# Attention stage: two accumulator banks, row maxima in three single banks with one VectorE instruction each, and the rounding of the maxima on GpSimd

## The reference

```
qkv    = (h @ w_qkv + b_qkv).reshape(B, T, 3, 16, 16)       # B=4, T=1024, 16 heads of 16 channels
scores = einsum('bhqd,bhkd->bhqk', q, k) / sqrt(16)
attn   = softmax(scores, axis=-1)
out    = einsum('bhqk,bhkd->bhqd', attn, v)
```

## Time and profile before

| | us |
|---|---|
| median of three runs (1148.0 to 1151.61) | 1149.8 |
| the profiled execution, its own time | 1148.59 |
| its span, first to last instruction | 1146.5 |
| PE busy in the span | 1062.9 (93%) |
| DVE busy | 997.4 (87%) |
| ACT busy | 808.4 (71%) |
| POOL busy | 244.1 (21%) |

### The profile page before, as it was taken

The page is one execution under the profiler, slowest core; times in us unless marked ns, Lnnn a source line. Parts: engine busy times, 40 slices in busy tenths (PEclk is TensorE's granted clock), DMA queues, the critical chain, the costliest instruction groups (busy, mean ns, idle before and its releaser), DMA issues.

```text
span 1146.5 us, 22167 instructions
## 1 busy us (share of the span) xinstructions
PE 1062.9 (93%) x8566; PEld 580.9 (51%) x8566; DVE 997.4 (87%) x1475; ACT 808.4 (71%) x1654; POOL 244.1 (21%) x345
## 2 busy tenths in 40 slices
PE   5997799999999999999999999997899998799995
PEld 4885233333333333333333333334667666788984
DVE  7776999999999999999999999943499988569887
ACT  4452188888888888888888888873578687243443
POOL 6413400000000000000000000102254424565643
PEclk9898599999999999999999999998999998899997
DMA  8595304404423441441343150211133325634321
GB/s 273 155 302 208 51 17 67 67 22 75 68 37 51 67 61 28 76 67 33 55 68 56 39 76 12 92 57 59 39 123 132 117 79 167 194 84 135 103 75 55
DMA packets 87333, 101.55 MB, mean 89 GB/s; under 512 B 21885, under 2 KB 57213, under 8 KB 87229
## 3 DMA queue, kind: packets, MB, share of 16 engines
q1 hardware_dynamic: 86396, 98.56, 36.1%
q10 hardware_dynamic: 832, 1.58, 0.4%
HBM read 55.09 MB, written 43.88 MB: 86 GB/s over the span
## 4 chain that ended last, share of the span: by engine, by line
PE 74%; DVE 8%; ACT 3%; issue 3%; POOL 1%; DMA 1%; SPq 0%; PEldq 0%; ACTq 0%; DVEq 0%; POOLq 0%
PE ps_o L799 25%; PE ps_s L787 19%; PE ps_m L776 10%; PE p_a L1344 3%; DVE maxes L726 3%; PE p_p L1416 2%; PE p_p L1770 2%; PE p_t L1350 1%; PE p_a L1747 1%; DVE zT_lo L2033 1%; PE p_p L1711 1%; ACT L1111 1%; PE p_p L1712 1%; PE p_t L1721 1%; PE p_t L1695 1%
## 5 line engine op out<-in xcount | busy, mean ns | idle before, releaser
L680 ACT ACTIVATE prob<-ps_s 128x512 f32<-128x512 f32 x1024 | 555.8, 597 | 118.1 <-PE ps_s L787 98.3
L726 DVE TENSOR_REDUCE maxes<-ps_m 128x2 f32<-128x1024 f32 x512 | 608.6, 1217 | 17.5 <-PE ps_m L776 14.0
L799 PE MATMUL ps_o<-prob,v_ones 128*32 128x256 f32 x4096 | 327.8, 392 | 8.1 <-issue 7.7
L787 PE MATMUL ps_s<-q_stack,k_stack 64*128 64x512 f32 x1024 | 260.5, 499 | 0.0
L776 PE MATMUL ps_m<-k_stack,q_stack 62*128 62x512 f32 x1024 | 216.6, 416 | 14.8 <-DVE maxes L726 11.1
L787 PEld LDWEIGHTS ps_s<-q_stack,k_stack 64*128 64x128 f32 x1024 | 99.0, 184 | 211.3 <-ACT prob L680 188.3
L799 PEld LDWEIGHTS ps_o<-prob,v_ones 128*32 128x32 f32 x4096 | 81.6, 108 | 196.2 <-ACT prob L680 99.5
L640 POOL COPY v_ones<-v_all 128x512 f32<-128x512 f32 x16 | 9.8, 614 | 528.7 <-PE ps_o L799 528.7
L776 PEld LDWEIGHTS ps_m<-k_stack,q_stack 62*128 62x128 f32 x1024 | 100.9, 192 | 27.5 <-DVE maxes L726 23.4
L407 ACT ACTIVATE p_parts<-ps_qk,cols 128x512 fp32r<-128x512 f32 x32 | 22.0, 687 | 39.8 <-PE ps_qk L452 32.1
L1416 PE MATMUL p_p<-p_hT,w_p 128*128 128x512 f32 x96 | 44.3, 612 | 2.6 <-ACT p_hT L1181 2.6
(11 more groups left out here) (301 smaller groups left out, 1536.9 us busy)
## 6 DMA issues: line engine op xcount, KB each, us to landing
qk_parts<-p_parts SPq DMA_DIRECT2D x32, 512.0 KB, 7.3
q_stack<-qk_parts SPq DMA_DIRECT2D x96, 128.0 KB, 4.7
k_stack<-qk_parts SPq DMA_DIRECT2D x96, 128.0 KB, 7.7
oT<-o_sb SPq DMA_DIRECT2D x32, 256.0 KB, 3.9
x_all<-in_x_dram SPq DMA_DIRECT2D x8, 512.0 KB, 10.1
heads<-oT SPq DMA_DIRECT2D x16, 256.0 KB
inverse<-inverse_sums SPq DMA_DIRECT2D x16, 256.0 KB
out_dram<-x_all SPq DMA_DIRECT2D x7, 512.0 KB, 3.4
```

What stands on the lines that cost most here:

```text
L680: act.activation(prob[at % P_RING][:, h], ps_s[:, (GH * at + h) % S_RING], ACT.Exp, scale=HD ** -0.5).then_inc(exp_done, 1)
L726: dve.tensor_reduce(maxes[:, i // 2, i % 2], ps_m[:, i % M_PAIRS], AX.X, ALU.max).then_inc(m_taken, 1)
L787: pe.matmul(ps_s[:, (GH * (UNITS * slot + KT * qc + kt) + h) % S_RING], r32(k_st[slot][rows, pair, kt * P:(kt + 1) * P]), r32(q_st[slot][r ...
L799: ins = pe.matmul(ps_o[32 * h:32 * h + 32, queries], v_st[slot][:, kt, h], prob[(UNITS * slot + KT * qc + kt) % P_RING][:, h, queries], st ...
```

## The change

`ps_o` gets two banks (`O_RING` = 2), one for each half `qc`, and `ps_m` three single banks (`M_RING` = 3) in place of four. TensorE's wait before the first `weigh` of a half is now for the copy of the half before the last one. The copy is made in two parts of 256 queries, behind the exponentials of `kt` 1 and `kt` 2 (`O_TAKEN_AT`). Each `score_for_max` product waits for its own bank and signals on its own, and each has its own `tensor_reduce` over 512 columns with a negated result, so a half has 32. The two halves of the keys are then combined by a minimum. The rounding and the remainder move to GpSimd (`negate`), but for the last two halves, where VectorE still does them; the transpose stays on VectorE (`turn`), behind the fourth reduce of the next half. GpSimd's other work is put between these steps in its list: a bias addition behind the steps of halves 2 to 9, a `place_v` in every second half.

```diff
+M_RING = 3
+O_RING = 2
+O_TAKEN_AT = (1, 2)
-BEHIND_LAST, BETWEEN = (0, 1), {0: (2, 3)}
+POOL_HALVES, TURN_BEHIND = QC * NG - 2, 3
...
-        ps_m = ctx.enter_context(nc.psum_tensor("ps_m", [P, M_PAIRS, 2, CHUNK], F32))
-        ps_o = ctx.enter_context(nc.psum_tensor("ps_o", [P, CHUNK], F32))
+        ps_m = ctx.enter_context(nc.psum_tensor("ps_m", [P, M_RING, CHUNK], F32))
+        ps_o = ctx.enter_context(nc.psum_tensor("ps_o", [P, O_RING, CHUNK], F32))
...
+        def negate(eng, half):
+            if half:
+                eng.wait_ge(m_turned, half)
+            eng.wait_ge(negated, 3 * half + 1)
+            eng.tensor_copy(r32(neg[:, 0]), least[:]).then_inc(negated, 1)
+            eng.wait_ge(negated, 3 * half + 2)
+            eng.tensor_tensor(neg[:, 1], least[:], neg[:, 0], ALU.subtract).then_inc(negated, 1)
...
-            for n in range(NCH):
-                at = x_all[:, TPC * n:TPC * n + TPC]
-                pool.tensor_tensor(at, at, rows[:, ROW_BOUT:ROW_BOUT + 1].to_broadcast([P, TPC, C]), ALU.add).then_inc(bias_added, 1)
-            for it in range(1, 5):
-                for u in range(3):
-                    place_v(3 * it + u, u)
-            place_v(NG - 1, 0)
+            for half in range(POOL_HALVES):
+                negate(pool, half)
+                if 2 <= half < 2 + NCH:
+                    at = x_all[:, TPC * (half - 2):TPC * (half - 2) + TPC]
+                    pool.tensor_tensor(at, at, rows[:, ROW_BOUT:ROW_BOUT + 1].to_broadcast([P, TPC, C]), ALU.add).then_inc(bias_added, 1)
+                g = half // QC + 1
+                if half % QC == 0 and SLOTS <= g < NG:
+                    place_v(g, g % SLOTS)
...
+            def take_o(g, qc, part):
+                if part == 0:
+                    act.wait_ge(pv_done, UNITS * g + KT * (qc + 1) + 2)
+                    act.wait_ge(o_out[qc], 16 * g)
+                queries = slice(part * CHUNK // 2, (part + 1) * CHUNK // 2)
+                act.activation(o_sb[qc][:, queries], ps_o[:, qc % O_RING, queries], ACT.Copy).then_inc(o_taken, 1)
...
-                        if kt == 0 and not (first and qc == 0):
-                            take_o(g - 1 if qc == 0 else g, 1 - qc)
+                        if kt in O_TAKEN_AT and not (first and qc == 0):
+                            take_o(g - 1 if qc == 0 else g, 1 - qc, O_TAKEN_AT.index(kt))
...
+            def turn(half):
+                dve.wait_ge(negated, 3 * half + 3)
+                dve.wait_ge(m_in[half % QC], 32 * (half // QC))
+                dve.transpose(negT[half % QC][:], neg[:].rearrange("p a b -> p (a b)")).then_inc(m_turned, 1)
...
             def maxima(g, qc):
                 half = QC * g + qc
-                for i in range(M_MMS // 2):
-                    dve.wait_ge(m_ready, M_MMS // 2 * half + i + 1)
-                    dve.tensor_reduce(maxes[:, i // 2, i % 2], ps_m[:, i % M_PAIRS], AX.X, ALU.max).then_inc(m_taken, 1)
-                    if half and i in BETWEEN:
-                        for step in BETWEEN[i]:
-                            negate(half - 1, step)
-                    if g == NG - 2 and i % 4 == 1:
-                        invert(4 * qc + i // 4)
-                for step in BEHIND_LAST if half < QC * NG - 1 else range(4):
-                    negate(half, step)
+                if half:
+                    dve.wait_ge(negated, 3 * half - 2)
+                for i in range(M_MMS):
+                    n = M_MMS * half + i
+                    dve.wait_ge(m_ready, n + 1)
+                    dve.tensor_reduce(maxes[:, i:i + 1], ps_m[:, n % M_RING], AX.X, ALU.max, negate=True).then_inc(m_taken, 1)
+                    if 0 < half <= POOL_HALVES and i == TURN_BEHIND:
+                        turn(half - 1)
+                    if g == NG - 2 and i % 8 == 3:
+                        invert(4 * qc + i // 8)
+                by_head = maxes[:].rearrange("p (hp t kc par) -> p hp t kc par", hp=HP, kc=2, par=2)
+                dve.wait_ge(negated, 3 * half)
+                dve.wait_ge(m_taken, M_MMS * (half + 1))
+                dve.tensor_tensor(least[:].rearrange("p (hp par t) -> p hp t par", hp=HP, par=2), by_head[:, :, :, 0], by_head[:, :, :, 1], ALU.min).then_inc(negated, 1)
+                if half >= POOL_HALVES:
+                    negate(dve, half)
+                    turn(half)
...
             def score_for_max(g, slot, qc, i):
-                n = M_MMS // 2 * (QC * g + qc) + i // 2
-                if i % 2 == 0 and not (isinstance(n, int) and n < M_PAIRS):
-                    pe.wait_ge(m_taken, n - M_PAIRS + 1)
+                n = M_MMS * (QC * g + qc) + i
+                if n >= M_RING:
+                    pe.wait_ge(m_taken, n - M_RING + 1)
...
                     if kt == 0:
-                        pe.wait_ge(o_taken, QC * g + qc)
+                        if QC * g + qc >= O_RING:
+                            pe.wait_ge(o_taken, 2 * (QC * g + qc - O_RING + 1))
```

More of the change, by code:

```diff
@@ L538, in attend @@
         prob = [sb(f"prob{i}", [P, GH, CHUNK]) for i in range(P_RING)]
-        maxes = sb("maxes", [P, M_MMS // 4, 2, 2])
-        maxm = sb("maxm", [P, M_MMS // 2])
+        maxes = sb("maxes", [P, M_MMS])
+        least = sb("least", [P, M_MMS // 2])
         neg = sb("neg_max", [P, 2, M_MMS // 2])
@@ L556, in attend @@
         o_taken, o_out = sem("o_taken"), [sem(f"o_stored{i}") for i in range(QC)]
-        own, bias_added = sem("vector_steps"), sem("out_bias_added")
+        negated, bias_added = sem("max_negated"), sem("out_bias_added")
         z = v_st[(NG - 3) % SLOTS][:].rearrange("p k g d -> p (k g d)").rearrange("p (i c) -> p i c", c=C)
@@ L690, in on_scalar @@
             group(NG - 1, 0)
-            take_o(NG - 1, 1)
+            take_o(NG - 1, 1, 0)
+            take_o(NG - 1, 1, 1)
         def on_vector(dve):
-            steps = Steps(dve, own)
             def invert(part):
@@ L699, in invert @@
                 dve.reciprocal(sums[:, at], sums[:, at]).then_inc(inverted, 1)
[L701 to L720, removed]
@@ L762, in on_vector @@
             scale, zT, zT_lo = const["ternary_scale"][:], rows_1["zT"], rows_1["zT_lo"]
-            dve.tensor_scalar(r32(zT[:]), ps_m[:, 0], scale, None, ALU.mult).then_inc(zT_ready, 1)
+            dve.tensor_scalar(r32(zT[:]), ps_m[:, 0:CH], scale, None, ALU.mult).then_inc(zT_ready, 1)
             dve.wait_ge(zT_ready, 1)
-            dve.scalar_tensor_tensor(out=r32(zT_lo[:]), in0=ps_m[:, 0], scalar=scale, in1=zT[:], op0=ALU.mult, op1=ALU.subtract).then_inc(rows_lowered, 1)
+            dve.scalar_tensor_tensor(out=r32(zT_lo[:]), in0=ps_m[:, 0:CH], scalar=scale, in1=zT[:], op0=ALU.mult, op1=ALU.subtract).then_inc(rows_lowered, 1)
         def on_tensor(pe):
@@ L770, in score_for_max @@
             def score_for_max(g, slot, qc, i):
[L771 to L773 removed]
+                n = M_MMS * (QC * g + qc) + i
+                if n >= M_RING:
+                    pe.wait_ge(m_taken, n - M_RING + 1)
                 hp, t, kc, base = i // 16, i // 4 % 4, i // 2 % 2, BASES[i % 2]
                 q0 = qc * CHUNK + t * P
[L776 to L779 removed]
+                pe.matmul(ps_m[:, n % M_RING], r32(q_st[slot][base:base + MROW, hp, q0:q0 + P]),
+                          r32(k_st[slot][base:base + MROW, hp, kc * CHUNK:(kc + 1) * CHUNK]), start=True, stop=True).then_inc(m_ready, 1)
             def score(g, slot, qc, kt, h):
@@ L795, in weigh @@
                     if kt == 0:
-                        pe.wait_ge(o_taken, QC * g + qc)
+                        if QC * g + qc >= O_RING:
+                            pe.wait_ge(o_taken, 2 * (QC * g + qc - O_RING + 1))
                         pe.wait_ge(v_set, g + 1)
                 for h in range(GH):
-                    ins = pe.matmul(ps_o[32 * h:32 * h + 32, queries], v_st[slot][:, kt, h],
+                    ins = pe.matmul(ps_o[32 * h:32 * h + 32, qc % O_RING, queries], v_st[slot][:, kt, h],
                                     prob[(UNITS * slot + KT * qc + kt) % P_RING][:, h, queries],
@@ L829, in begin_mixing @@
                 if i < TPC:
[L830 removed]
+                    ins = pe.matmul(ps_m[:, i // 2, i % 2 * C:(i % 2 + 1) * C], heads["o"][0][:, c, i * P:(i + 1) * P], const["w_out"][:, c],
                                     start=c == 0, stop=c == CH - 1)
@@ L836, in begin_mixing @@
                     for j in range(TPC):
-                        ins = pe.transpose(ps_m[:, 0, c, j * P:(j + 1) * P], z[:, j, c * P:(c + 1) * P], const["ident"][:])
+                        ins = pe.transpose(ps_m[:, c, j * P:(j + 1) * P], z[:, j, c * P:(c + 1) * P], const["ident"][:])
                     if c == CH - 1:
```

18 lines of the change are left out of this document (4 added, 14 removed).

## The result

The changed kernel takes 1156.43 us (median of 6 runs, 1155.21 to 1160.17) where the kernel before takes 1149.49 on the same chip: a ratio of 1.0075, with a 95% interval of 1.0056 to 1.0094. It is 0.75% slower by that ratio; the two medians as they stand lie 6.9 us, 0.60%, apart. The profiled execution took 1159.8 us, with a span of 1157.7. Two executions of kernels further down, of 1576.74 and 1985.69 us, were far slower than the others of the same kernel and are left out of the medians.

The account below looks back on a forecast made before the run. TensorE's list was taken to set the pace, plus 0.30 us a half waiting for the accumulator. Terms -9.3 + 4.8 + 9.0 + 2.4 + 2.8 = +9.7 on 1148.6, plus 1.2 for a median, gave 1159 us; range 1140 to 1185.

Parts of the forecast that it names:

- The accumulator's wait: TensorE's wait for the accumulator's copy before a half's first `weigh`: 0.30 us removed from each of 31 halves, -9.3 us.
- The two copies at nothing: On ScalarE, copying the accumulator as two pieces of 256 columns: 0.24 us each, covered up to 0.02, taken as 0.
- A reduce of 0.68 us, 0.592 apart: On VectorE, each 512-column reduce: 0.68 us long, 0.592 from start to start, 18.9 us in a half.
- The ring of three: A slot's second product for the maxima waits for its bank: 0.02 us late, settling at 0.01 a slot, +4.8 us.
- The step between halves: Next half's first reduce waits for the minimum, delaying TensorE: 0.30 us at each of 30 ends of a half, +9.0 us.
- The transpose: On VectorE behind the fourth reduce: 0.14 us less 0.06 left over in a slot, 30 x 0.08 = +2.4 us.
- The reciprocals: Eight on VectorE, in two halves, no longer absorbed by its room: 0.46 us each, +2.8 us in all.
- Before the pace is set: First 48 products on VectorE's pace: +1.3 us, against up to -2.1 if the 2.25 us step goes; taken as 0.
- spare time at the ring: Rival: TensorE's second product finds its bank free early, so delays shrink; faster, 1145 to 1140.5 us; chance 0.31.
- s: Spare time in us before a slot's second product needs its bank, taken off each delay; decides the sign from 0.08.

## Why the prediction was right

It said 1159 and slower, by delays that reach TensorE through a ring without spare time; that is what the runs show. Its sum for the profiled execution was +9.7 us, and it was +11.2; the medians lie 6.9 apart. That the sum came so near is in part luck: the ring and the step between halves were set too low by 1.8 and about 2 us, the block and the start of the stage (+0.6 and +1.0) were missed, and against that the transpose's 2.4 and 0.6 of the reciprocals' 2.8 didn't come. By its steps:

- *The accumulator's wait, -0.30 a half.* Right: no long slot is left, and giving the wait back costs 0.26 a half and 10 us in all (one accumulator, three banks).
- *The two copies at nothing.* Right: with the other costs off, a half is 19.83.
- *A reduce of 0.68 us, 0.592 apart.* Right: 0.684 and 0.598. Against 1.131 for 1024 columns that leaves 2 x 0.598 - 1.131 = 0.065 us for an instruction's fixed part. The prediction weighed about 125 ns for it, from the Trainium skill's Perfetto Trace Analysis (Optimizing Scalar/DVE Operations); for reduces back to back this trace doesn't agree, and the half of 20.15 with four single banks shows that the split cost a plain half nothing.
- *The ring of three, 0.01 a slot, +4.8 us.* The mechanism was right, the size half as large again: 0.0147 a slot, 0.22 a half, about +6.6. Two banks make the same gate plain.
- *The step between halves, +0.30.* Right in place and releaser, mis-sized: 0.38, about +11. The prediction let the minimum start 0.04 behind the last reduce, as before. That reduce ends at 411.12 + 2.52 = 413.64, and the minimum starts at 413.75, 0.11 behind it: 0.07 of the 0.08 that was missing.
- *The transpose, +0.08.* Not there: its slot is 1.24. So not every delay on VectorE reaches TensorE. I take it that TensorE, held in the slot before, asks for its next bank later than the transpose makes it free; no run takes this apart.
- *The reciprocals, +2.8.* +2.6 over plain halves, less the 0.42 that they cost before: +2.2. It fell on three halves (21.12, 21.75 and 21.06), not on two near 22.
- *Missed:* the block of four steps on VectorE, +0.6 in one half. The prediction said that rounding leaves VectorE, and passed over the two halves that keep it.
- *Before the pace is set, 0.* From the first reduce to the first copy the trace has 56.38 against 52.90 us, 2.51 of it because the copy's first part is one key tile, two slots, later: +1.0, though the 2.25 us step has gone. Its parts weren't taken apart.

Together, from traces: +7.5 in 25 plain halves, +3.0 in the three with reciprocals (0.87 and 2.2), +0.9 in the next one, +1.0 ahead, and -0.7 in what is left of the attention: +11.7. The stretches ahead of and behind the attention have -0.5, which makes the +11.2. The profiled execution lay 3.4 us above its median, and that of the kernel before 0.9 below, so the medians differ by less than this.

Of the rivals, spare time at the ring is what reduces of 448 columns create (s is there, and the kernel becomes faster, 0.9943); with 512 columns it wasn't there. It was close: 0.07 us on a reduce turns the sign.

## What to carry to other kernels

Before taking a bank from a ring, follow one bank round: product, reduce, the way back, next product. Here both engines still fitted by their sums, and the half became longer because in every other slot a product needed a bank some 0.03 us before it was free (1.27 against 1.24). Once a ring has no spare time, a small step for which the consumer stops between two reads can be paid in full by the producer (the minimum, 0.38 us a half), so put such steps behind the first work of the next stage, with a second buffer: there the minimum cost next to nothing, and the transpose among the reduces cost nothing that the slots show. A step moved off an engine that has room buys nothing: with four banks taking the rounding off VectorE was worth 0 a plain half, with three the block of rounding, remainder and transpose cost 0.6.

## What the runs showed of the hardware that was not expected

The first rounding of maxima on VectorE, a tensor_scalar with fp32r output of 16 columns, took 2.25 us before; the same instruction later in that trace (429.83) and, in the kernel with the steps back on VectorE, a cast of the same size at the same place (124.31) took 0.17. What made the first one slow stays open.

When the second of two side-by-side products for the maxima waits, the pair takes 0.78 us (414.44) instead of 0.40, and a wait of 0.33 on the weights goes with a slot that is 0.38 longer.

The round trip of the maxima through DRAM took from 735.01 to 742.89 where its store came 5.6 us behind the last of eight loads, and 1.97 us where it came 10.4 behind. TensorE's wait of 1.43 us for it cost some 3.0 over three slots (2.78, 1.77 and 2.17), as the granted clock was 0.50 behind it.
